# A two-layer gated cross-attention kernel on one core: first keys with VectorE's operations spread over four groups, first queries and second keys in one block

## What is computed

```python
# first layer: queries, keys, values on integer grids
q = x_normed @ Wq + bq                 # 2048 rows, 16 heads of 16
k, v = cond @ Wkv + bkv                # 12808 rows
q = fq_sym(q * 0.25, axis=-1); k = fq_sym(k, axis=-1)   # scale: max |.| / 127 in each head of a row
v = fq_sym(v, axis=rows)
# second layer: keys and values as they are, batch by batch
k, v = split(cond @ wkv.T + bkv)       # attention is within a batch of 1601 rows
```

## Time and profile before

| | us |
|---|---|
| runs | 6532.99, 6537.80, 6538.09 |
| median | 6537.8 |
| profiled execution | 6530.62 |
| span of its trace | 6528.6 |
| first queries with setup | 0 to 110.7 |
| first keys | 110.7 to 483.9 |
| first values, then first attention | from 483.9, from 583.6 |
| second queries, second keys | to 5228.1, to 5447.9 |

### The profile page before, as it was taken

One profiled execution on the slowest core, in us unless ns is written; L12 is line 12 of the kernel. 1 busy time (PEld: TensorE's weight loads), 2 busy tenths in 40 slices (PEclk: granted clock), 3 DMA queues, 4 the chain that ended last, 5 costly groups with the idle time before them and its releaser, 6 DMA issues. The chain is left out here.

```text
span 6528.6 us, 180102 instructions
## 1 busy us (share of the span) xinstructions
PE 5668.4 (87%) x64160; PEld 2228.2 (34%) x64160; DVE 5520.5 (85%) x8987; ACT 4504.5 (69%) x4373; POOL 3787.3 (58%) x4002
## 2 busy tenths in 40 slices
PE   2874999999999999999999999999969487999823
PEld 2651233333233233233233323323344353544412
DVE  4877999999999999899999989999953556777786
ACT  0660499999899899899889989989932012666512
POOL 2331488888888888888888888888820001000031
PEclk7995799999999999999999999999979797999956
DMA  1544101101101001011011011010010078777600
GB/s 60 130 121 129 17 7 27 20 9 27 19 11 25 15 16 25 10 21 23 10 24 20 9 28 18 11 26 15 15 37 1 21 302 198 117 109 114 104 28 12
DMA packets 176565, 315.50 MB, mean 48 GB/s; under 512 B 91731, under 2 KB 137812, under 8 KB 171042
## 3 DMA queue, kind: packets, MB, share of 16 engines
q1 hardware_dynamic: 175656, 303.45, 21.7%
HBM read 192.39 MB, written 113.07 MB: 47 GB/s over the span
## 5 line engine op out<-in xcount | busy, mean ns | idle before, releaser
L1182 DVE TENSOR_REDUCE a_mx<-PS 128x1 f32<-128x512 f32 x6620 | 3985.0, 682 | 212.4 <-PE PS L1066 208.8
L1153 ACT ACTIVATE a_e<-PS,a_sk 126x1024 f32<-126x1024 f32 x3264 | 3633.9, 1114 | 377.9 <-PE PS L1049 128.5
L920 POOL TENSOR_SCALAR a_p<-a_e 126x1024 f16<-126x1024 f32 x3264 | 3418.4, 1047 | 560.0 <-ACT a_e L1153 180.7
L1066 PE MATMUL PS<-a_K,a_Q 48*128 48x512 bf16 (+1 forms) x6884 | 2104.3, 382 | 30.6 <-POOL a_K L885 30.3
L1093 PE MATMUL PS<-a_e,a_sel 126*32 126x256 f32 x26112 | 1988.8, 381 | 29.2 <-issue 29.2
L1049 PE MATMUL PS<-a_Q,a_K 54*128 54x512 bf16 x6528 | 1976.7, 383 | 32.9 <-issue 23.6
L1089 PE MATMUL PS<-a_p,a_V 128*32 128x256 f16 x13056 | 958.2, 283 | 14.8 <-POOL a_p L920 9.9
L1049 PEld LDWEIGHTS PS<-a_Q,a_K 54*128 54x128 bf16 x6528 | 369.3, 94 | 1383.3 <-issue 1320.7
L1089 PEld LDWEIGHTS PS<-a_p,a_V 128*32 128x32 f16 x13056 | 336.5, 93 | 1342.7 <-issue 1253.7
L1093 PEld LDWEIGHTS PS<-a_e,a_sel 126*32 126x32 f32 x26112 | 754.7, 110 | 38.0 <-issue 31.2
L2139 DVE TENSOR_REDUCE b_mx<-PS 128x1 f32<-128x512 f32 x803 | 504.7, 684 | 186.7 <-PE PS L2023 186.7
(11 more groups left out here) (322 smaller groups left out, 3521.2 us busy)
## 6 DMA issues: line engine op xcount, KB each, us to landing
b_K<-d_k SPq DMA_DIRECT2D x210, 200.1 KB, 6.3
a_K<-d_k SPq DMA_DIRECT2D x99, 400.2 KB
d_v<-v1v SPq DMA_DIRECT2D x9, 3328.0 KB, 10.4
b_V<-d_v SPq DMA_DIRECT2D x36, 832.0 KB, 12.3
d_k<-k_T SPq DMA_DIRECT2D x100, 252.0 KB, 4.0
d_k<-k1p SPq DMA_DIRECT2D x54, 400.2 KB, 7.4
a_V<-d_v SPq DMA_DIRECT2D x68, 204.0 KB, 2.7
d_v<-vq SPq DMA_DIRECT2D x17, 803.2 KB
```

The lines of the kernel that those rows point to most:

```text
L920: g.tensor_scalar(p[0:rows, kk % RE, :], e[0:rows, kk % RE, :], 1.0, SHIFT, ALU.mult, ALU.add).then_inc(rounded, 1)
L1066: last = pe.matmul(self.PS[:, M_BANK + j % sh.SLOTS, c0:c0 + wd], Qb[M_ROWS, ii % 4, t * P:(t + 1) * P], Kb[M_ROWS, (ii // NC) % 2, k0:k0 ...
L1153: a.activation(e[0:r, kk % RE, :], self.PS[0:r, e_bank(i, s):e_bank(i, s) + 2, :], ACT.Exp, scale=skb[0:r, hb, s:s + 1]).then_inc(exp_done, 1)
L1182: v.tensor_reduce(mx[:, col:col + 1], bank, AX.X, ALU.max).then_inc(max_done, 1)
```

## The change

- `setup`, `first_queries` and `second_keys` become one block at the start, `first_queries_second_keys`. PE runs the eight batches of second keys, key chunks and value tiles alternating, and between them what the queries need: the transposes of x after batch 1, the query projection after batch 2, the transposes of the query parts after batch 5.
- In that block ScalarE takes out key chunks (twice: f32 and the first bf16 part) and value tiles, and makes the middle part; GpSimd makes the two subtractions of each chunk; VectorE works on the queries alone. The value bias is a third matmul of three bf16 rows. Key parts have one buffer a half, values a ring of three quarter batches, PSUM rings are of two banks.
- Keys of a half batch are stored in one DMA, values by quarters. The spare batch is copied from DRAM to DRAM, after batch 3's stores. The query parts are stored after batch 6's.
- In `first_keys`, `parts` and `ip` get rings of four. VectorE's operations each signal with their own increment, wait for a semaphore of the operation that they need, and work on groups g to g - 3 in turn. PE's transposes lag four groups behind the projection, ScalarE's evacuation five. The memset of 32 partitions of `v_raw` goes, and `first_values` works on 126 partitions of it.

```diff
             self.sems = self.early
-            self.setup()
-            self.first_queries()
+            self.first_queries_second_keys()
...
-            self.second_keys()
...
+            kf = self.sb(ctx, "k1f", [P, 3, BANK])
+            kt = self.sb(ctx, "k1t", [P, 2, BANK])
+            kp = self.sb(ctx, "k1p", [P, 2, 3, LK], BF16)
+            vv = self.sb(ctx, "v1v", [P, 3, TQ, HEADS, 2 * HD])
...
+            def batch_order(b):
+                done = 0
+                for i, key in enumerate(key_jobs(b)):
+                    yield "key", key
+                    while done * KJ < (i + 1) * KT1:
+                        yield "value", (b * KT1 + done, done)
+                        done += 1
...
+            STORE_ORDER = (("v", 0), ("v", 1), ("k", 0), ("v", 2), ("v", 3), ("k", 1))
...
+                sp.dma_start(W1[:, :, :], w["L1_xattn_wkvT"].rearrange("(c p) n -> p c n", p=P)).then_inc(ld_w, 16)
+                load(0)
...
+                sp.dma_start(self.x[:, :, :], w["x"].rearrange("b (t p) d -> p (b t) d", p=P)).then_inc(ld_x, 16)
...
+                for b in range(NB):
+                    for kind, i in STORE_ORDER:
+                        if kind == "k":
+                            sp.wait_ge(k_low, b * KJ + (i + 1) * NC1)
+                            sp.dma_start(self.d_k1[:, b, 8 * i:8 * i + 8].rearrange("i h d n -> (h d) i n"),
+                                         kp[:, i, :, :]).then_inc(k_stored[i], 16)
+                        else:
+                            t0, t1 = QUARTERS[i]
+                            slot = (4 * b + i) % SLOTS
+                            sp.wait_ge(v_taken, b * KT1 + t1)
+                            sp.dma_start(self.d_v1[b, :, t0 * 2 * D:t1 * 2 * D],
+                                         vv[:, slot, 0:t1 - t0, :, :].rearrange("p t h d -> p (t h d)")).then_inc(v_stored[slot], 16)
+                    if b + 2 < NB:
+                        load(b + 2)
+                    if b == 3:
+                        for m in range(2):
+                            sp.wait_ge(k_stored[m], 16)
+                        for i in range(SLOTS):
+                            sp.wait_ge(v_stored[i], 16 * (1 + (i == 0)))
+                        for i in range(3):
+                            sp.dma_start(self.d_k1[i, NB], self.d_k1[i, 0]).then_inc(spare, 16)
+                        sp.dma_start(self.d_v1[NB], self.d_v1[0]).then_inc(spare, 16)
+                    if b == NB - 2:
+                        sp.wait_ge(pT_taken, 16)
+                        sp.dma_start(self.d_sq[:, 0:HEADS, :], sqs[:, :, :]).then_inc(q_stored, 16)
+                        for i, part in enumerate(PART_ORDER):
+                            for c in range(2):
+                                sp.dma_start(self.d_q0[part, 8 * c:8 * c + 8].rearrange("h d n -> (h d) n"),
+                                             turned_parts[i][:, c, :]).then_inc(q_stored, 16)
...
+                def low(j, m, k0, wd):
+                    g.wait_ge(k_mid, j + 1)
+                    g.tensor_tensor(kp[:, m, 2, k0:k0 + wd], kt[:, j % 2, 0:wd], kp[:, m, 1, k0:k0 + wd], ALU.subtract).then_inc(k_low, 1)
...
+                for b in range(NB):
+                    for j, m, k0, wd in key_jobs(b):
+                        g.wait_ge(k_taken, j + 1)
+                        if j >= 2:
+                            g.wait_ge(k_low, j - 1)
+                        g.tensor_tensor(kt[:, j % 2, 0:wd], kf[:, j % 3, 0:wd], kp[:, m, 0, k0:k0 + wd], ALU.subtract).then_inc(k_rest, 1)
+                        if last:
+                            low(*last)
+                        last = (j, m, k0, wd)
...
+                def keys(b, j, m, k0, wd):
+                    if j >= 2:
+                        pe.wait_ge(k_taken, j - 1)
...
+                    pe.matmul(self.PS[0:n, 2 + j % 2, 0:D], pick[0:96, 0:n], bp[0:96, :], start=False, stop=True).then_inc(v_ps, 1)
...
+                    for kind, job in batch_order(b):
+                        if kind == "key":
+                            keys(b, *job)
+                        else:
+                            values(b, *job)
+                    if b == 1:
+                        turn_x()
+                    if b == 2:
+                        queries()
+                    if b == 5:
+                        turn_parts()
...
+                def middle(j, m, k0, wd):
+                    a.wait_ge(k_rest, j + 1)
+                    a.activation(kp[:, m, 1, k0:k0 + wd], kt[:, j % 2, 0:wd], ACT.Copy).then_inc(k_mid, 1)
...
+                def key_chunk(b, j, m, k0, wd):
+                    a.wait_ge(k_ps, j + 1)
+                    if j >= 3:
+                        a.wait_ge(k_rest, j - 2)
+                    if b >= 1 and k0 == 0:
+                        a.wait_ge(k_stored[m], 16 * b)
+                    a.activation(kf[:, j % 3, 0:wd], self.PS[:, j % 2, 0:wd], ACT.Identity, bias=bk[:, m:m + 1])
+                    a.activation(kp[:, m, 0, k0:k0 + wd], self.PS[:, j % 2, 0:wd], ACT.Identity,
+                                 bias=bk[:, m:m + 1]).then_inc(k_taken, 1)
+                def value_tile(b, j, t):
+                    n = value_rows(t)
+                    q = [t0 <= t < t1 for t0, t1 in QUARTERS].index(True)
+                    t0, (use, slot) = QUARTERS[q][0], divmod(4 * b + q, SLOTS)
+                    a.wait_ge(v_ps, j + 1)
+                    if t == t0 and use >= 1:
+                        a.wait_ge(v_stored[slot], 16 * use)
+                    a.activation(vv[0:n, slot, t - t0, :, 0:HD], self.PS[0:n, 2 + j % 2, 0:D].rearrange("p (h d) -> p h d", d=HD),
+                                 ACT.Copy).then_inc(v_taken, 1)
...
+                        key_chunk(b, *job)
+                        if last:
+                            middle(*last)
+                        last = job
...
-            RC = 6
+            RC, RP = 6, 4
...
-                    if g >= 2:
-                        turn(g - 2)
-                turn(NG - 2)
-                turn(NG - 1)
+                    if g >= 4:
+                        turn(g - 4)
+                for g in range(NG - 4, NG):
+                    turn(g)
...
-                g.memset(self.v_raw[96:P, :, :], 0.0).then_inc(zeroed, 1)
...
+                def over(g, op, signal):
+                    todo = spans(g)
+                    for s, n in todo[:-1]:
+                        self.link(v, op(s, n), self.dv)
+                    op(*todo[-1]).then_inc(signal, 1)
...
+                def largest_key(g):
                     v.wait_ge(kv_ready, g + 1)
+                    over(g, lambda s, n: v.tensor_reduce(scale_of(g, s, n), by_head(keys_of(g, s, n)), AX.X, ALU.max,
+                                                         apply_absolute_value=True), k_largest)
+                def scale(g):
+                    v.wait_ge(k_largest, g + 1)
+                    over(g, lambda s, n: v.tensor_scalar(scale_of(g, s, n), scale_of(g, s, n), 1.0 / 127.0, 1e-8, ALU.mult, ALU.max), k_scale)
+                def reciprocal(g):
+                    v.wait_ge(k_scale, g + 1)
                     if g >= 2:
                         v.wait_ge(ip_ready, g - 1)
+                    over(g, lambda s, n: v.reciprocal(rk[0:n, g % 2, s, :], scale_of(g, s, n)), rk_ready)
+                def multiplied(g):
+                    v.wait_ge(rk_ready, g + 1)
+                    if g >= 2:
+                        v.wait_ge(k_whole, g - 1)
+                    over(g, lambda s, n: v.tensor_tensor(by_head(tmp[0:n, g % 2, s, :]), by_head(keys_of(g, s, n)),
+                                                         along(rk[0:n, g % 2, s, :], 3, HD), ALU.mult), kv_seen)
+                def whole(g):
+                    v.wait_ge(kv_seen, g + 1)
+                    if g >= RP:
+                        v.wait_ge(parts_T, g - RP + 1)
+                    over(g, lambda s, n: v.tensor_scalar(parts[0:n, g % RP, INT, s, :], tmp[0:n, g % 2, s, :], ROUND, ROUND,
+                                                         ALU.add, ALU.subtract), k_whole)
+                def scaled(g):
+                    v.wait_ge(k_whole, g + 1)
+                    if g >= 2:
+                        v.wait_ge(to_middle, g - 1)
+                    over(g, lambda s, n: v.tensor_tensor(by_head(kf[0:n, g % 2, s, :]), by_head(parts[0:n, g % RP, INT, s, :]),
+                                                         along(scale_of(g, s, n), 3, HD), ALU.mult), to_high)
                 def rest(g):
+                    v.wait_ge(high_done, g + 1)
+                    if g >= 2:
+                        v.wait_ge(parts_ready, g - 1)
+                    over(g, lambda s, n: v.tensor_tensor(tmp2[0:n, g % 2, s, :], kf[0:n, g % 2, s, :], parts[0:n, g % RP, HI, s, :],
+                                                         ALU.subtract), to_middle)
+                def last(g):
+                    v.wait_ge(middle_done, g + 1)
```

(60 more changed lines are left out.)

462 lines of the change are left out of this document (223 added, 239 removed).

## The result

The changed kernel takes 6460.07 us (median of four runs, 6455.1 to 6466.4), the kernel before 6535.95 (four runs, 6532.99 to 6538.09). The ratio is 0.9885, with a 95% interval of 0.9868 to 0.9902: 76 us less. The profiled execution of after is the slowest of its four, 6466.4 us with a span of 6464.5.

What follows compares the result with a forecast made beforehand. Second keys was taken as bound by PE, first keys as a loop through three engines with neither VectorE nor PE full. -24.6 - 42.5 + 2.2 = -64.9 us from 6530.6 gives 6465.7, put 2 up to 6468; range 6430 to 6500.

Steps and rivals of the forecast that it cites:

- Head of first keys: Opening of first keys: the 21.85 us memset goes, larger rings add 3.8 us; 39.2 us becomes 21.1.
- Loop: First keys' groups: VectorE's operations overlap, three engines set 12.26 us for two groups, 6.13 each; 298.9 us against 312.4.
- Tail: End of first keys: four groups under way instead of two, so 28.6 us instead of 21.7.
- Joint block: First queries and second keys together, reckoned by PE: 288.0 us in place of 330.5, so -42.5 us.
- Lock: Joint block: VectorE's long query operations hold up GpSimd's subtractions and behind them PE; +13 us, bounds 5 and 25.
- Copy: Batch 4 of the joint block: value stores wait in SP's queue behind the spare batch's 5.87 MB; 18 us plus 2 for clock.
- its first rival: Joint block: the copy shares engines with the stores and GpSimd is let in between, so no stands; 6434 us, chance 0.18.
- Semaphore clearing: Opening of first attention: GpSimd clears 68 early semaphores instead of 34; +2.2 us.
- the 6.42 loop: Rival in first keys: VectorE's operations do not overlap, 6.42 us a group, 16 us missing; 6484 us, chance 0.18.
- The longer stands: Rival in the joint block: 30 us instead of 18 for the copy, 25 instead of 13 for GpSimd; 6492 us, chance 0.12.
- PE's clock: Rival in the joint block: at 1.2 GHz a 24.4 us batch nearly becomes 48.8; 6655 us with all eight, chance 0.04.
- a sign of a wrong base: Joint block: PE's granted clock below 0.8 over whole batches would make the sum wrong at its base.

Runs made afterwards that it cites:

- the runs with own waits: Each VectorE operation of first keys waits for its own signal before the next: in the kernel after 6499.96 us; with PE's transposes five groups behind, 6435.82 us.
- the lag of five: Kernel after with PE's transposes in first keys five groups behind the projection instead of four: 6406.83 us (ratio 0.9797).
- the chain cut: Kernel after with the seven large operations of VectorE's query chain each cut into four of 1024 elements: 6447.26 us (ratio 0.9854).

## Why the prediction was right

It said 6468 us, range 6430 to 6500; measured 6460. By stages it had -64.9 us, and the traces show -73.3. The 8.4 between are a joint block 10.3 and a loop 4.4 shorter than forecast, less 6.3 for the head, the tail, the clearing and first values; that they partly cancel is luck, and so is that the price of the copy, worked out from order in a queue, came within 4 us. Term by term:

- **Head of first keys**: 21.1 forecast, 22.0 measured. The memset's exit is confirmed by the run that put it back.
- **Loop**: the mechanism was right, both its halves shown: operations overlap (0.61 for 0.69, and the runs with own waits), and the loop goes through VectorE, ScalarE's evacuation and PE (the lag of five opens it). 12.26 us forecast for two groups, 12.08 measured, as 6.80 and 5.28 in turn and not evenly; 298.9 forecast for the whole loop, 294.5 measured (299.66 to 594.15). The earlier trace rows decided rightly between two readings of the Trainium skill: its page "VectorE: DVE Perf Modes", section "The DRAIN you can't avoid", measures that a signal after each operation costs nothing, and its section "Rules for kernel authors" advises fewer operations and not fewer semaphores. The first of these sections also says that "a next op that is not held starts earlier", which the prediction left out, and the 0.61 us step agrees with that. Here a wait for one's own signal costs 0.11 us an operation, 1.0 us for the nine of a group; if the flush always held the next operation, the runs with own waits would have shown no difference, and they show 29 and 40 us. Signals without waits, which the page timed, were not tried alone.
- **Tail**: 28.6 forecast, 31.3 measured. PE's transposes in the tail, behind 2.40 us of idle time (6.21 before the first), take 1.84 us and not the 1.04 of the earlier trace rows that I used.
- **Joint block**: 288.0 forecast, 277.7 measured. Reckoned by PE (first matmul 12.80, last one's end 268.43), with the prices of batches 3 and 4 taken from the intervals between stores: start 15.5 (forecast 13.6; the first matmuls took 3.75 us where they later take 1.88); eight batches of 23.9 are 191.2 (195.1); the queries' work of PE 17.2 (20); turned parts 8.5 (10.8); lock 16.3 (13); copy 16.1 (20); query stores 3.6 (6); tail 9.2 (9.5). The base and four smaller prices were each set 2 to 4 us too high, the start and the lock too low. Split by the end of PE's own batches, the lock is 13.2 and the copy 18.5, with 0.7 in batch 5; the sum is the same. The bare batch was mis-sized first: 24.4 us from 22.96 of the earlier trace rows and 1.4 for the bias matmuls; the trace shows 23.9.
- **Lock**: confirmed as a lock by length of instruction. The page "SBUF — State Buffer" of the Trainium skill, section "SBUF: two separate sides", says that a VectorE operation with two SBUF inputs, or one in a 2-port mode, and a GpSimd instruction hold one port pair in turn, each for the whole instruction. The trace agrees for two inputs, in both directions: VectorE's multiplications and subtractions became 5.19 to 5.26 us long where the earlier trace rows has 4.43. Part of the price is PE's clock, granted at 0.87 in batch 3 and at 1.00 there with the chain cut.
- **Copy**: the size was near (20 forecast, 16.1 measured), the reason mostly wrong. The prediction gave the stand to SP's queue, "one queue, in order of issue", and its first rival, 6434, was that the copy shares the engines with the stores and nothing stands. Both tied the stand to the order, and that is the step that failed: on a second queue 11.4 of the 16.1 us of batch 4 stay, with 1.6 new in batch 3. For the rival I had read the earlier trace rows wrongly: a DMA share of 0.77 in the mean of second keys' window is no room for 5.9 MB inside one batch, which moves its own bytes at the same time.
- **Semaphore clearing**: +2.2 forecast, +2.5 measured. First values were not in the sum and cost 2.4.
- **Rivals**: the 6.42 loop appears when the overlap is taken away, in every second pair of groups; in the others the clock makes it longer. The longer stands (30 and 25) did not come. PE's clock is a real danger: it fell to 0.87 and 0.79 in batches 3 and 4, but a batch never took twice its time. The 0.79 is below the 0.8 that the prediction named as a sign of a wrong base; the base held (batch 6 took 23.9 us), and the low clock came with the 13.9 us in which PE stood in batch 4.

What I undervalued is not in the sum: the loop of 12.26 us was worked out, with its members, and I did not ask what one group more of lag would do to it. That edit alone is worth 53 us, where the pipeline without it brought some 4.

## What to carry to other kernels

Once a loop goes through several in-order engines, write down its members and move one of them an iteration away. While the loop is closed every member's time counts, as the own waits show (0.89 us a group); when it is open the longest engine sets the period. Long VectorE operations beside a GpSimd that others wait for should be cut in pieces. A large copy holds up the stores beside it on whichever queue it is; spread in pieces over several batches it cost nothing here, even where the transfer engines were busy.

## What the hardware showed that I had not expected

- A second queue does not take away a stand: 5.9 MB from DRAM to DRAM on ScalarE's queue took 20.9 us for its last piece to land, 23.2 on SP's, and ScalarE still waited 16 us in that batch for stores of SP's queue.
- PE falls to the lower clock after some short waits and not after others, and the longer wait isn't always the one: 16 transposes took 1.04 us behind 1.68 us of waiting in after and behind 2.78 in the run with own waits, but 1.84 behind 2.29 in that same run and behind 2.40 in the tail.
- The first matmuls of the kernel took 3.75 us for four where later ones take 1.88, though the window 12 to 17 us shows a granted clock of 1.00. That 1.00 says nothing: the trace's record of the clock begins at 18.4 us, and the window 0 to 12, in which PE does nothing, shows 1.00 too. The matmuls are slow up to 18.3 us and at their later pace from there on, which fits the lower level at the start.
- VectorE's operations with one input meet the lock too. With the chain cut in four, eleven of its twelve one-input operations of 1024 elements began inside a subtraction of GpSimd, and all eleven ended 0.54 to 0.57 us after it: eight that began early in it took 1.53 to 1.59 us, as the one at 132.01 beside the subtraction of 130.84, and three that began in its last 0.13 us took 0.69. In after the 4096-wide ones at 118.25 and 127.05 took 3.13 and 3.07 us, where the kernel before has 2.29. No run without GpSimd's work was made.
